# A four-layer graph network on one core: destinations and attention row read from PSUM, one-hot pieces interleaved over two chains, two banks merged, three steps moved

## The reference

```
g      = leaky_relu(xl[src] + xr[dst] + edge_attr @ W_e, 0.2)     # xl, xr: two products of h
logits = einsum('ehc,hc->eh', g, att)                             # 4 heads of 16 channels
ex     = exp(logits - segment_max(logits, dst)[dst])
alpha  = ex / (segment_sum(ex, dst)[dst] + 1e-16)
out    = segment_sum(xl[src] * alpha, dst) + bias                 # then batch norm, gelu
```

## Time and profile before

| what | us |
|---|---|
| median of 3 runs | 6286.97 (6284.62 to 6289.7) |
| the profiled execution | 6286.53 |
| its span (first to last instruction) | 6284.9 |
| `segment_ends` to the end of `expand_rows` | about 13 to 372 |
| `edge_loop` | about 372 to 2690 |
| the layers after it | from there to the end |

### The profile page before, as it was taken

One profiled execution on the slowest core, in us unless ns is written; L12 is line 12 of the kernel. 1 busy time (PEld: TensorE's weight loads), 2 busy tenths in 40 slices (PEclk: granted clock), 3 DMA queues, 4 the chain that ended last, 5 costly groups with the idle time before them and its releaser, 6 DMA issues. The chain is left out here.

```text
span 6284.9 us, 115432 instructions
## 1 busy us (share of the span) xinstructions
PE 4956.5 (79%) x35178; PEld 4246.0 (68%) x35178; DVE 2990.8 (48%) x4364; ACT 1854.1 (30%) x3935; POOL 3748.4 (60%) x3427
## 2 busy tenths in 40 slices
PE   2448888888888888824999957877788887884899
PEld 2335666666656666613999957777787777784899
DVE  7768888888888888737222121111111111112321
ACT  0025555555555555500000012222222222221100
POOL 7677777777777777740000047777777777776000
PEclk9668888888888888856999955555555555555799
DMA  9335555555555555523999756666667666664698
GB/s 359 104 106 160 161 162 155 159 154 158 158 157 161 155 153 161 143 49 132 367 366 365 278 157 195 208 205 210 202 197 209 206 209 208 200 200 110 254 402 327
DMA packets 622991, 1260.53 MB, mean 201 GB/s; under 512 B 131705, under 2 KB 431290, under 8 KB 597220
## 3 DMA queue, kind: packets, MB, share of 16 engines
q10 hardware_dynamic: 206000, 595.93, 30.4%
q1 hardware_dynamic: 307508, 546.42, 24.1%
q0 software_dynamic: 109184, 115.05, 8.6%
HBM read 923.85 MB, written 490.51 MB: 225 GB/s over the span
## 5 line engine op out<-in xcount | busy, mean ns | idle before, releaser
L733 POOL DMA_INDIRECT att_gl<-tab_l,top_zero x1568 | 1801.4, 1149 | 488.5 <-issue 476.1
L1217 POOL DMA_INDIRECT sum_gl<-tab_l,top_zero x1568 | 1547.1, 987 | 517.9 <-issue 477.6
L970 ACT ACTIVATE att_acc<-att_pc 128x392 bf16<-128x392 f32 x2352 | 1085.5, 497 | 1113.3 <-PE att_pc L751 984.5
L748 PE MATMUL att_pc<-att_ohl,att_ohv 128*128 128x392 bf16 x2352 | 849.1, 361 | 216.5 <-DVE att_ohl L849 216.3
L1145 PE MATMUL sum_pm<-sum_msg,sum_S 128*128 128x64 f32 x3136 | 672.2, 408 | 399.2 <-ACT sum_msg L1185 399.2
L1145 PEld LDWEIGHTS sum_pm<-sum_msg,sum_S 128*128 128x128 f32 x3136 | 646.0, 316 | 432.4 <-ACT sum_msg L1185 219.3
L751 PE MATMUL att_pc<-att_acc,att_ohv 128*128 128x392 bf16 x2352 | 843.2, 359 | 117.8 <-ACT att_acc L970 114.4
L1115 DVE TENSOR_TENSOR sum_t<-sum_pb,sum_gl 128x512 f32<-128x512 f32 x196 | 135.6, 692 | 1664.6 <-DMA sum_gl<-tab_l,top_zero 1293.8
L1127 PE MATMUL sum_pb<-sum_wbs,sum_ea 64*128 64x64 f32 x3136 | 694.8, 419 | 29.1 <-DMA sum_ea<-in_ea64T 29.1
L1127 PEld LDWEIGHTS sum_pb<-sum_wbs,sum_ea 64*128 64x128 f32 x3136 | 676.2, 329 | 40.9 <-DMA sum_ea<-in_ea64T 29.5
L767 PEld LDWEIGHTS att_pl<-att_xe,att_S 128*128 128x128 f32 x3136 | 588.0, 213 | 149.0 <-issue 125.2
(11 more groups left out here) (384 smaller groups left out, 5260.5 us busy)
## 6 DMA issues: line engine op xcount, KB each, us to landing
A<-att_acc SPq DMA_DIRECT2D x2352, 98.0 KB
l_a<-A SPq DMA_DIRECT2D x147, 1568.0 KB, 9.2
att_dall<-in_dst ACTq DMA_DIRECT2D x224, 448.0 KB
sum_dall<-in_dst ACTq DMA_DIRECT2D x196, 512.0 KB, 5.0
hop_at<-AT SPq DMA_DIRECT2D x56, 1568.0 KB
sum_a<-A ACTq DMA_DIRECT2D x49, 1568.0 KB
AT<-sum_at ACTq DMA_DIRECT2D x49, 1568.0 KB, 6.4
l_at<-AT SPq DMA_DIRECT2D x42, 1568.0 KB
```

Of the source, the lines that this page charges most:

```text
L733: nc.gpsimd.indirect_dma_start(out=gl[s][:, k * GQ + j, :], out_offset=None, in_=g.tab_l, in_offset=bass.IndirectOffsetOnAxis(ap=g.ix[:, c ...
L748: nc.tensor.matmul(pc[c][m % 2][:, 0:LO], ohv[c][h][:, m, :, 0], ohl[c][h][:, m // 2, :, m % 2], start=True, stop=False)
L970: nc.scalar.activation(acc[c][n % CR][:, :], pc[c][m % 2][:, 0:LO], ACT.Copy).then_inc(s_acc[c], 1)
L1217: nc.gpsimd.indirect_dma_start(out=gl[n % RB][:, j, :], out_offset=None, in_=g.tab_l, in_offset=bass.IndirectOffsetOnAxis(ap=g.ix[:, c:c + ...
```

## The change

All in the stages up to the end of `edge_loop`.

1. **PSUM.** The transposes move from their own bank `pt` into the sums' bank `pm`; the bank that comes free is `pk`, written and read by VectorE alone. It holds `k_att` (the attention row, copied once) and `k_dst` (two halves of 28 columns: the destinations of a block, copied a block ahead by the new `own_ends`). `S` and the multiplication in `logits` take these as their second operand, instead of `dst` and `att` in SBUF. `S` waits for the copy (`s_kd`) in k = 0.
2. **Sharing the bank.** `scores` now waits until the sums of the block two back are emptied (`s_ev`) and moves from k = 0, m = 4 to k = 1, m = 0. The `sums` of the third and fourth quarter move from k = 0 and 1 to k = 0 alone, `keep_sums` with them.
3. **Items.** The one-hots of a chain are made in two pieces (first pair, then the rest), and first pieces of both chains come before the second pieces of both. `ohv`, one instruction before, becomes two; the six instructions of a step become eight.
4. **Degrees.** `ohl` of 3584 elements is made in two halves.
5. **ScalarE in `segment_ends`.** `root` comes before `windows`.
6. **SyncE in `expand_rows`.** The load for the degrees comes after the release of the scatters.

```diff
@@ Degrees.one_hots
-                    v.tensor_tensor(
-                        t[k][:, :, :, :], spread(c[:, :, :].unsqueeze(1), [P, J // 2, w, 2]),
...
+                    pieces = ((0, J // 4), (J // 4, J // 2)) if t is self.ohl else ((0, J // 2),)
+                    for a, z in pieces:
+                        ins = v.tensor_tensor(
+                            t[k][:, a:z, :, :], spread(c[:, :, :].unsqueeze(1), [P, z - a, w, 2]),
...
+                    ins.then_inc(self.s_oh, 1)
@@ segment_ends, scalar
+                root(act)
                 act.wait_ge(s_ck, 1)
                 item_rows.windows(act)
-                root(act)
@@ expand_rows, sync
-            degrees.load(sp)
             sp.wait_ge(g.s_zero, 16 * (ZR + 2))
             sp.sem_inc(s_ix, 1)
+            degrees.load(sp)
@@ edge_loop
-        pt = st.ps("pt", [P, 512])
+        pk = st.ps("pk", [P, 512])
         pm = st.ps("pm", [P, 512])
+        pt = pm
+        k_att, k_dst = pk[:, 0:D], pk[:, D:D + SL * GQ]
@@ tensor
                 def scores(b, s):
                     wait_reuse(pe, s_xb, b)
+                    wait_reuse(pe, s_ev, b * NQ)
...
-                            if k == 0 and m == 4 and first:
+                            if k == 1 and m == 0 and first:
                                 scores(b - 1, 1 - s)
...
-                            if k < 2 and second and m in (0, 1):
-                                sums(b - 2, s, 2 + k, range(0, 4) if m == 0 else range(4, GQ))
+                            if k == 0 and second and m in (0, 1, 3, 4):
+                                sums(b - 2, s, 2 + m // 3, range(0, 4) if m % 3 == 0 else range(4, GQ))
@@ vector
+                    if k == 0:
+                        dve.wait_ge(s_kd, i * R + (s + 1))
                     v.tensor_tensor(S[s][:, k * GQ:(k + 1) * GQ, :], dall[k][:, :, :],
-                                    spread(dst[:, bass.ds(i * (R * GB) + t * GQ, GQ)].unsqueeze(2), [P, GQ, P]),
+                                    spread(k_dst[:, t * GQ:(t + 1) * GQ].unsqueeze(2), [P, GQ, P]),
...
+                def own_ends(i, s):
+                    v.tensor_copy(k_dst[:, s * GB:(s + 1) * GB],
+                                  dst[:, bass.ds(i * (R * GB) + s * GB, GB)]).then_inc(s_kd, 1)
...
-                    step(v.tensor_tensor(t2[:, :, :], t2[:, :, :], spread(att[:, :].unsqueeze(1), [P, GQ, D]),
+                    step(v.tensor_tensor(t2[:, :, :], t2[:, :, :], spread(k_att.unsqueeze(1), [P, GQ, D]),
...
-                        for c in range(CH):
-                            items(i, t, c)
+                        for a, z in ((0, 1), (1, SLOTS[t] // 2)):
+                            for c in range(CH):
+                                items(i, t, c, a, z)
...
+                        if k == NQ - 1 and not (isinstance(i, int) and i == TURNS - 1 and s == R - 1):
+                            own_ends(i if s == 0 else i + 1, 1 - s)
@@ scalar
-                            if k < 2 and second and m == 3:
-                                keep_sums(b - 2, s, 2 + k)
+                            if k == 0 and second and m in (2, 5):
+                                keep_sums(b - 2, s, 2 + m // 3)
```

More of the change, by code:

```diff
@@ L380, in turn @@
                         dve.wait_ge(self.s_hm, i * R + (k + 1 - R))
-                    v.tensor_tensor(
-                        t[k][:, :, :, :], spread(c[:, :, :].unsqueeze(1), [P, J // 2, w, 2]),
-                        spread(x[:, bass.ds(i * (R * J) + k * J, J)].rearrange("p (j two) -> p j two", two=2).unsqueeze(2),
-                               [P, J // 2, w, 2]), ALU.is_equal).then_inc(self.s_oh, 1)
+                    pieces = ((0, J // 4), (J // 4, J // 2)) if t is self.ohl else ((0, J // 2),)
+                    for a, z in pieces:
+                        ins = v.tensor_tensor(
+                            t[k][:, a:z, :, :], spread(c[:, :, :].unsqueeze(1), [P, z - a, w, 2]),
+                            spread(x[:, bass.ds(i * (R * J) + (k * J + 2 * a), 2 * (z - a))]
+                                   .rearrange("p (j two) -> p j two", two=2).unsqueeze(2), [P, z - a, w, 2]),
+                            ALU.is_equal)
+                    ins.then_inc(self.s_oh, 1)
         repeat(dve, self.HALF // (R * J), turn)
@@ L694, in edge_loop @@
             "S", "pl", "t1", "L", "LT", "sub", "exp", "back", "xb", "exm", "msg", "sum", "ev", "top"))
-        s_ends = st.sem("ends")
+        s_ends, s_kc, s_kd = (st.sem(k) for k in ("ends", "kc", "kd"))
         s_out = [st.sem(f"out{s}") for s in range(R)]
@@ L842, in items @@
+                def items(i, t, c, a, z):
+                    h = t % 2
                     n0 = i * (CB * CJ) + (c * CI + at0[t])
-                    if not known(i, 1) or t >= 2:
+                    if a == 0 and (not known(i, 1) or t >= 2):
                         dve.wait_ge(s_mm[c], i * (CB * CJ) + (at0[t - 1] if t >= 2 else (-SLOTS[SL - 1], 0)[t]))
-                    v.tensor_tensor(ohv[c][h][:, 0:w, :, :], spread(c_row2[:, :, :].unsqueeze(1), [P, w, P, 2]),
-                                    spread(g.vals[:, bass.ds(n0, w), :].unsqueeze(2), [P, w, P, 2]), ALU.is_equal)\
-                        .then_inc(s_oh[c], 1)
@@ L848, in items @@
-                    for a, z in ((0, 1), (1, w // 2)):
-                        v.tensor_tensor(ohl[c][h][:, a:z, :, :], spread(c_lo2[:, :, :].unsqueeze(1), [P, z - a, LO, 2]),
-                                        spread(g.lo[:, bass.ds(n0 + 2 * a, 2 * (z - a))]
-                                               .rearrange("p (j two) -> p j two", two=2).unsqueeze(2),
-                                               [P, z - a, LO, 2]), ALU.is_equal).then_inc(s_oh[c], 1)
+                    v.tensor_tensor(ohv[c][h][:, 2 * a:2 * z, :, :],
+                                    spread(c_row2[:, :, :].unsqueeze(1), [P, 2 * (z - a), P, 2]),
+                                    spread(g.vals[:, bass.ds(n0 + 2 * a, 2 * (z - a)), :].unsqueeze(2),
+                                           [P, 2 * (z - a), P, 2]), ALU.is_equal).then_inc(s_oh[c], 1)
@@ L854, in logits @@
+                    v.tensor_tensor(ohl[c][h][:, a:z, :, :], spread(c_lo2[:, :, :].unsqueeze(1), [P, z - a, LO, 2]),
+                                    spread(g.lo[:, bass.ds(n0 + 2 * a, 2 * (z - a))]
+                                           .rearrange("p (j two) -> p j two", two=2).unsqueeze(2),
+                                           [P, z - a, LO, 2]), ALU.is_equal).then_inc(s_oh[c], 1)
                 def logits(i, n, b, s, k):
@@ L909, in turn @@
                             logits(i - 1, i * SL + (-1), b - 1, 1, NQ - 1)
+                        if k == NQ - 1 and not (isinstance(i, int) and i == TURNS - 1 and s == R - 1):
+                            own_ends(i if s == 0 else i + 1, 1 - s)
+                v.tensor_copy(k_att, att[:, :]).then_inc(s_kc, 1)
+                own_ends(0, 0)
+                dve.wait_ge(s_kc, 1)
                 turns(dve, TURNS, turn)
```

6 lines of the change are left out of this document (2 added, 4 removed).

## The result

The changed kernel takes 6316.4 us (median of 12 runs, 6296.1 to 6323.6) against 6277.1 for the kernel before in the same session: ratio 1.0057, 95% interval 1.0049 to 1.0066. The forecast was 6155 in a range of 6075 to 6240; the kernel got slower, so the sign is wrong too. The profiled run took 6312.5 us (span 6310.8). Ratios, here and in the table of experiments, are not the quotients of the medians beside them; that of e3_early also leaves out its longest run (6273 us).

What follows compares the result with a forecast made beforehand. It took GpSimd's gathers, held up by VectorE instructions with two SBUF operands, as the bound. Savings of 97 us in the loop, 13 from root first and 21 from scatters sum to 131: 6286.5 becomes 6155, range 6075 to 6240.

Steps and rivals of the forecast that it cites:

- The gathers: Loop, GpSimd: with PSUM operands, `S` and the `att` multiplication stop holding gathers; 0.60 and 0.195 us a step go.
- The pieces of `ohv`: Loop, VectorE: splitting `ohv` lowers its holding of gathers from 0.75 to 0.53 us a step before scaling by 0.70.
- The pace of 77.9: Loop: 9.74 us a step, 77.9 a turn instead of 81.4; 97 us less if GpSimd stays the bound.
- Does it stay the bound?: Loop: VectorE's work of 72.5 us a turn leaves 5.4 for waits that take 7.6; GpSimd was to stay the bound.
- the interleaved pieces: Loop, one-hots: earlier first pieces start TensorE 0.5 to 1.9 us earlier, to close a gap of 2.2 us a turn.
- the moved `scores`: Loop, k = 1: the wait for ScalarE's emptying of the sums costs nothing, covered by an item copy TensorE awaits anyway.
- The fourth rival: Loop: late transposes make VectorE wait in `softmax`; at 3 us a block, 86.1 a turn, 98 us more, 6384; chance 0.07.
- threshold of 1.3 us a block: Loop, `softmax`: the wait for scores from which the fourth rival was to decide, on top of 80.1 us a turn.
- Ahead of the loop: Stages before the loop: root first saves 13 us and the scatters 21, 34 together.
- root: `segment_ends`: root before the windows lets VectorE start about 20.6 us earlier, its reciprocal at about 43 us; net 18.4.
- weights: Next stage: weights queued behind zero-filling until about 178.5 hold TensorE's product to about 179.5; 13 us less, 18 at most.
- scatters: `expand_rows`: release 6 us earlier, 1.87 us a scatter beside the degrees; stage ends some 21 us earlier.

Runs made afterwards that it cites:

- e3_early: Changed kernel with three quarters of the sums in k = 3, one in k = 0, and scores back in k = 0; 6247 us, ratio 0.9885 to before.
- e10: e6 with `S` and the `att` multiplication reading their second operand from SBUF again; 6283 us, ratio 0.9994 to the kernel before.
- e6: Changed kernel with two of VectorE's four message multiplications moved from k = 2 to k = 3; 6141 us, ratio 0.9776 to the kernel before.
- e14: e6 with VectorE's one-hots in the order and pieces of the kernel before; 6159 us, ratio 0.9788 to the kernel before.
- e5: Changed kernel with the attributes' matmul ahead of the items at the head of k = 3, done three times; 6150 us, ratio 0.9788 to before.
- e13: Changed kernel with VectorE's one-hots in the order and pieces of the kernel before; 6287 us, ratio 1.0004 to the kernel before.
- e9: Changed kernel with the attributes' matmul ahead of the items at the head of k = 3, done once; 6181 us, ratio 0.9825 to before.
- e2: Kernel before with only `scores` moved from k = 0 to the head of k = 1; 6338 us, ratio 1.0103 to the kernel before.
- e11: Kernel before with only the messages split over k = 2 and k = 3; 6243 us, ratio 0.9926 to the kernel before.
- e12: Changed kernel with e3_early's sums and scores, e6's split messages, and weights ahead of the loop on ScalarE's queue; 6117 us, ratio 0.9724 to before.
- e15: e12 with the attributes' matmul ahead of the items as in e9; 6127 us, ratio 0.9737 to the kernel before.

## Why the prediction was wrong

**The gathers: right, and under-rated.** `S` and the multiplication by `att` hold no gather any more and did not get longer; the mean of 1074 is 12 ns from the forecast's 1086. The forecast took the two for 0.795 x 7 / 9.7 x 0.70 = 0.40 us a step; e10 against e6 shows (2289.6 - 2149.5) / 224 = 0.63. The pieces of `ohv`, taken for 0.11 a step, gave nothing (e14). What the Trainium skill reports (SBUF — State Buffer, Who interferes with whom: a probe in which `tensor_tensor` did not stall a DMA issued from GpSimd) does not hold for these instructions: in e10 they cost 140 us of the loop. The forecast passed over the rule that stands beside this report in the Trainium skill, by which a VectorE instruction with two inputs in SBUF contends with a GpSimd instruction that reads SBUF, and one with at most one, outside the two-port modes, does not; e6 and e10 bear that out.

**The pace of 77.9: right while GpSimd is the bound.** It is seen in the first four turns, and in e5 throughout (77.3 on the mean, 6150 us in all). That this is only 5 us off the forecast is in part luck: e5's loop gives 116 us where 97 were forecast, and what stands ahead of it 24 where 34 were.

**"Does it stay the bound?" is the step that failed.** The forecast set VectorE's work and waits against 77.9, found 2.2 us a turn too much, and counted on the interleaved pieces to bring them. They bring nothing (e13, e14). And it costed the moved `scores` at nothing, covered by an item copy that TensorE waits for anyway. Cover there was none in the slow pace: TensorE comes to k = 1 late, not early (busy for 11.54 of the last 11.58 us ahead of the scores), and VectorE waits 2.74 us a block. How much of the lateness is the half clock from k = 3 on, how much the doubled sums in k = 0 and how much the later place is not shown; in e14 the wait is 2.05 us with the clock at 0.94. TensorE then lacks one-hots at the next k = 3, and in three blocks of four its pause there is followed by the next half-clock stretch. The forecast had read the pieces apart (TensorE's slow stretches, its wait of 5.0 in the earlier trace rows, VectorE's waits) and did not ask whether one feeds the other.

The fourth rival had the place right. Its formula gives 80.1 + 2 x 2.74 = 85.6 a turn; the slow turns, two by two, take 83.6. But its threshold of 1.3 us a block is not borne out: e14 waits 2.05 us a block and e9 some 1.9, and their turns are 76.8 and 77.9. So the wait alone does not set the pace, and the rival had no ring in it.

**What is shown of the ring, and what is open.** Shown: work put into TensorE's pause (e9), work and doubled work (e5), or 1.1 us out of VectorE's stretch ahead of it (e6) each bring the loop back to 77 to 78 on the mean, with the scores in their late place in all three. Late scores in the kernel before are enough to start it (e2). Early scores alone only put it off (e3). So edits at the pause at the head of k = 3 cut it, and the late scores are one way into it. Open: how much of the slow pace is the half clock, for no run changes the clock alone. In the changed kernel it is at 0.83 on the mean, but its first and third turns ran at 78.1 and 77.1 with the same clock, and e13 was slow at 0.90. No run has the doubled sums without the late scores, so what they add is open too. Open as well what ends the fast pace at the fifth turn here and at the tenth in e3.

**Ahead of the loop: root right, weights wrong, scatters right.** VectorE's reciprocal runs at 41.29 (forecast 43). The product was to start at 179.5, when the weights are there; it started at 189.46, so 3.7 us were gained there, not 13. The step read the end of the zero-filling from a DMA share, and did not see that the weights' own issue on that queue takes 8.40 us from 164.31, and that TensorE waits for them until 189.46. Behind that, the remaining 16.6 of the 20.3 us came in where 21 were forecast: GpSimd starts its scatters 9.7 us earlier (3.7 of it the product's, 6 as forecast the release's), and 32 of them beside the degrees take 1545 ns on the mean (forecast 1.5 to 1.7 us, 2314 in the earlier trace rows). Some of this is chance: with the same code ahead of it, the loop starts between 376.5 and 383.4 us in the three traces of the old order (before, e2, e11) and between 359.7 and 367.7 in the twelve of the new one (e12 and e15 aside).

```profile
164.31 8.40 SPq L258 DMA_DIRECT2D tab_ws<-in_L_Wlr  x1
...
219.93 2.77 POOL L600 DMA_INDIRECT xe<-tab_res,tab_sc_row  x1 [26.71 <-DVE tab_sc_row L585]
...
L600 POOL DMA_INDIRECT xe<-tab_res,tab_sc_row x32 | 49.5, 1545 | 9.8 <-issue 9.8
```

**A term that was not there.** With GpSimd ahead of the others, the loop ends 13.6 us later behind its last gather: the forecast took the end of the gathers for the end of the loop. This belongs to the slow pace as well: in e5 and e6, where GpSimd is the bound, the stretch is 39.7 and 43.9 us long, against 40.5 before and 54.1 here.

## What to carry to other kernels

When the bound of a loop is lifted, the other engines' waits for each other are the next bound, and they are to be added up round the ring (who is late because of whom, one lap later), not engine by engine against a mean. Before moving a step behind another, look whether the engine that issues it arrives there early or late; TensorE behind a pause was late for 16 us. And where two engines starve each other, the cheap cure is at the point where one runs dry: put work there that has to be done anyway (e9), or shorten what the other does just ahead of it (e6).
